# Reordering the turn of a feed-forward stage and taking the second stage's row sums in attention

## The reference

```python
x = x + 0.5 * ffn(layernorm(x))
x = x + attention(layernorm(x))       # causal softmax of |q.k|/16
x = x + 0.5 * ffn(layernorm(x))

def ffn(x):                           # the same weights in both stages
    m = k0 * x[row-1] + k1 * x + k2 * x[row+1]
    h = m @ W1[p] + b1[p]             # 9 paths, 64 wide each
    y = h @ W2[p] + b2[p]
    pick = argmax(tanh(m @ Wo1 + bo1) @ Wo2 + bo2)
    return layernorm(x + y[pick]) * gamma + beta
```

## Time and profile before

| | |
|---|---|
| time, median of 3 | 1526.47 us (1524.82 to 1528.2) |
| the profiled execution's own time | 1531.81 us |
| its span, first to last instruction | 1530.0 us |
| mean granted TensorE clock | 0.967 of full |
| busy: PE, DVE, ACT, POOL | 1359.1, 1215.7, 936.8, 306.9 us |
| chain that ended last: PE, DVE, DMA, ACT | 62%, 11%, 10%, 6% |

### The profile page before, as it was taken

The page is one execution under the profiler, slowest core; times in us unless marked ns, Lnnn a source line. Parts: engine busy times, 40 slices in busy tenths (PEclk is TensorE's granted clock), DMA queues, the critical chain, the costliest instruction groups (busy, mean ns, idle before and its releaser), DMA issues.

```text
span 1530.0 us, 25980 instructions
## 1 busy us (share of the span) xinstructions
PE 1359.1 (89%) x7700; PEld 781.4 (51%) x7700; DVE 1215.7 (79%) x2349; ACT 936.8 (61%) x1745; POOL 306.9 (20%) x359
## 2 busy tenths in 40 slices
PE   4889988858999999999968999999998779989985
PEld 2556666544554454545344455454444346656653
DVE  6989999766677677677866767777678769999985
ACT  5656665326567666566855666766666666666642
POOL 2244452332001000000041101000000214444311
PEclk9989999979999999999989999999999879999997
DMA  5143333320000100102110011000103112333221
GB/s 155 43 118 88 90 101 113 90 69 1 28 29 15 41 14 15 32 11 74 37 43 1 28 42 42 0 28 0 42 0 110 56 32 61 103 97 106 61 74 57
DMA packets 86994, 82.26 MB, mean 54 GB/s; under 512 B 8540, under 2 KB 86885, under 8 KB 86885
## 3 DMA queue, kind: packets, MB, share of 16 engines
q1 hardware_dynamic: 86884, 80.91, 17.8%
HBM read 55.43 MB, written 25.46 MB: 53 GB/s over the span
## 4 chain that ended last, share of the span: by engine, by line
PE 62%; DVE 11%; DMA 10%; issue 7%; ACT 6%; SPq 2%; POOL 1%; DVEq 0%; ACTq 0%; POOLq 0%
PE PS L1324 55%; DMA R<-oh_scratch 7%; PE PS L1501 3%; DMA oh_scratch<-oh_t 2%; DVE R L753 2%; PE PS L1389 2%; PE PS L1332 1%; DVE R L770 1%; DVE R L937 1%; SPq L414 1%; SPq L412 1%; ACT oh_t L1113 1%; ACT R L1211 1%; ACT R L1215 1%; ACT R L1174 1%
## 5 line engine op out<-in xcount | busy, mean ns | idle before, releaser
L1324 PE MATMUL PS<-R 128*128 128x512 f16 (+3 forms) x3456 | 713.6, 361 | 27.4 <-DVE R L937 17.3
L1324 PEld LDWEIGHTS PS<-R 128*128 128x128 f16 (+1 forms) x3456 | 326.0, 98 | 392.3 <-DVE R L937 32.0
L1324 PE MATMUL PS<-w_hi,R 128*128 128x256 f16 x1280 | 239.1, 280 | 63.3 <-DVE R L753 63.1
L937 DVE TENSOR_TENSOR R<-R 128x512 f16<-128x512 f32 (+3 forms) x288 | 188.6, 655 | 111.5 <-ACT R L1215 110.3
L1202 ACT ACTIVATE R<-PS 128x512 f32 (+5 forms) x288 | 160.2, 558 | 162.7 <-PE PS L1324 162.2
L1324 PE MATMUL PS<-R,w_hi 128*128 128x512 f16 x640 | 198.0, 392 | 1.6 <-DVE R L747 1.5
L1211 ACT ACTIVATE R<-R 128x512 f32 (+4 forms) x288 | 169.5, 589 | 48.3 <-DVE R L931 46.8
L931 DVE TENSOR_TENSOR R<-R,max_row 128x512 f32 (+4 forms) x288 | 187.1, 650 | 7.7 <-ACT max_row L1248 7.7
L1215 ACT ACTIVATE R<-R 128x512 f16<-128x512 f32 (+3 forms) x288 | 171.1, 594 | 28.6 <-ACT R L1211 2.6
L925 DVE TENSOR_TENSOR run_max<-run_max,R 128x512 f32<-128x512 f32 (+3 forms) x272 | 173.9, 639 | 10.0 <-DVE run_max L925 1.7
L1324 PEld LDWEIGHTS PS<-w_hi,R 128*128 128x128 f16 x1280 | 128.4, 100 | 104.5 <-DVE R L753 77.1
(11 more groups left out here) (109 smaller groups left out, 1555.3 us busy)
## 6 DMA issues: line engine op xcount, KB each, us to landing
R<-x_scratch SPq DMA_DIRECT2D x48, 512.0 KB, 4.5
x_scratch<-R SPq DMA_DIRECT2D x32, 512.0 KB, 3.2
R<-oh_scratch SPq DMA_DIRECT2D x32, 320.0 KB
R<-in_L_attn_x SPq DMA_DIRECT2D x16, 512.0 KB, 5.4
R<-oh_scratch SPq DMA_DIRECT2D x32, 256.0 KB
out<-R SPq DMA_DIRECT2D x16, 512.0 KB, 3.2
R<-in_L_ffn_W SPq DMA_DIRECT2D x2, 288.0 KB
R<-in_L_ffn_W SPq DMA_DIRECT2D x1, 512.0 KB
```

The lines of the kernel that those rows point to most:

```text
L937: v.tensor_tensor(p_lo[:, i * TT + lo:(i + 1) * TT], pf[:, (i % 2) * TT + lo:(i % 2 + 1) * TT], p_hi[:, i * TT + lo:(i + 1) * TT], ALU.sub ...
L1324: ins = t_.matmul(dst, w, xx, start=start and n == 0, stop=stop and n == last, skip_group_check=skip)
```

## The change

There are three edits.

1. The turn of a feed-forward stage is written in another order on every engine. The router's hidden product moves to the end of the turn before (`FIRST = ROUTE + 1`), so `route` is first on TensorE, and the five route steps on VectorE follow `result`, with the mixing passes between them. The masking of chunks 0, 1, 2 and 3 comes behind the route, each low half two chunks later. In the first stage the input sums stand in the middle of the turn. On ScalarE `scores` goes ahead of `middle`, and `one_hot` ahead of `x_high` and the masked high halves.
2. `residual` on GpSimd is for tile t instead of t+1, stands first in the turn, and waits for the paths of the tile before (`o_psum`) instead of for `masked`.
3. The sums of the second feed-forward stage's input rows are taken in attention (`output_sums`, one or two behind each `output`), into a buffer of their own, `x2_st`; the stage's turns only make the moments from them.

The masks get two semaphores, one for each of the two buffers.

```diff
+FIRST = ROUTE + 1
 # order of the hidden products
-                h_order += [(use(ph, t + ROUTE), 0)] if on(t + ROUTE) else []
                 h_order += [(use(ph, t + HIDDEN), c) for c in range(1, HC)] if on(t + HIDDEN) else []
+                h_order += [(use(ph, t + FIRST), 0)] if on(t + FIRST) else []
 # GpSimd, residual(t) and turn(t)
-                    pool.wait_ge(hm_done, HC * k + 4)
+                    if t >= 1:
+                        pool.wait_ge(o_psum, k)
...
+                    if on(t):
+                        residual(t)
                     if on(t - 1):
                         result_scale(t - 1)
-                    if on(t + HIDDEN):
-                        residual(t + HIDDEN)
 # VectorE, turn(t): the order after the change
+    result(t-1); route 0; mixed_before 0; route 1; mixed_before 1; route 2
+    mixed_behind 0; route 3; mixed_behind 1; route 4
+    masked 0; masked 1; input_sum x4 (first stage only); masked 2; mixed_low
+    masked 3; masked_low 0; masked 4; input_moments or first_stats
+    result_scaled(t-1); masked_low 1; masked_low 2; result_added(t-1)
 # and before
-    result(t-1); masked 0; masked 1; mixed_before 0; mixed_before 1; route 0
-    masked_low 0; route 1; masked 2; route 2; mixed_behind 0; route 3
-    mixed_behind 1; route 4; masked 3; input_sums or first_stats; mixed_low
-    masked 4; input_moments; masked_low 1; result_scaled(t-1); masked_low 2
-    result_added(t-1)
 # ScalarE, turn(t): after
+    scores; middle; squares; normalised; one_hot; x_high
+    masked_high 0; masked_high 1; masked_high 2; transposed
 # and before
-    middle; scores; masked_high 0; squares; normalised; x_high; one_hot
-    masked_high 1; transposed; masked_high 2
 # TensorE, turn(t): after
+    route(t+2); hidden(t+1, 1); path 0; hidden 2; path 1; choice(t+2); hidden 3
+    path 2; hidden 4; path 3; transposed(t+5); hidden(t+3, 0); path 4
 # and before
-    hidden(t+2, 0); hidden(t+1, 1); path 0; route(t+2); hidden 2; path 1
-    hidden 3; path 2; choice(t+2); transposed(t+5); hidden 4; path 3; path 4
 # VectorE, moments in the second stage, and output in attention
+                    dve.wait_ge(x2_sums, SUB * NTT)
+                    dve.wait_ge(n_shift, n - 1)
+                    for u in range(SUB):
+                        ins = v.bn_aggr(mv[:, rows_set(ph, t), u, :], sums_at(t, u))
...
+                    if u >= 1:
+                        output_sums(s, u - 1, rows)
+                    if u == SUB - 1:
+                        output_sums(s, u, rows)
+
+                def output_sums(s, u, rows):
+                    dve.wait_ge(x2_done, SUB * s + u + 1)
+                    v.bn_stats(sums_at(s, u), cols(rows, u * D, D)).then_inc(x2_sums, 1)
 # SyncE stores a row of attention, and TensorE, ScalarE and GpSimd start the
 # second stage, once x2_sums (before: x2_done) is complete
-            wait_apart(eng, x2_done, SUB * NTT)
+            wait_apart(eng, x2_sums, SUB * NTT)
```

## The result

The change made the kernel slower: 1533.15 us (median of 20 runs, 1529.82 to 1536.7) against 1527.12 for the kernel before on the same chip (20 runs, 1522.04 to 1536.35). The ratio is 1.0035, 95% interval 1.002 to 1.005. The forecast was 11.3 us less and the measured change is 6.0 us more, so 17 us are missing.

What follows compares the result with a forecast made beforehand. VectorE was taken to bound the feed-forward turns, TensorE attention. Stage one -1.0, attention +5 and stage two -15.3 sum to -11.3 us: 1515 against the median 1526.5, range 1490 to 1533.

Steps and rivals of the forecast that it cites:

- Bounds and hold: Feed-forward turns are bound by VectorE; residual's hold moves from mixed_low to the first mixed_before, costing 1.63 us.
- Is such a SCALAR_TENSOR_TENSOR held as the TENSOR_TENSOR was?: Whether residual holds the first mixed_before at the turn's start; taken as held, 1.63 us, bounds 0 and 2.36.
- The first: Rival: the first mixed_before is not held by residual, turns near 15.65 to 15.9 us, 1492 us in all; 14%.
- the second: Rival: residual gets the ports between two masked lows, L811 or L770 waits 2.3 us, 1538 us; 9%.
- The third: Rival: attention's sums lie on the path, two thirds of 21 us, no gain in starts, 1527 us; 11%.
- order alone saves only the 0.16 gap: VectorE's turn: the work is the same, so reordering removes only the 0.16 us gap before masked 3.
- The start gains about 1 net: Start of stage one: masks no longer bind, less 1 to 2 us lost in the first routing turn.
- -2.5: Start of stage two: the first path starts 2 to 3 us earlier, as VectorE routes instead of awaiting the mask.
- gain about 1 each: Stage one's two last turns with a residual: no mix to be held back, about 1 us less each.
- attention +5: Sums moved into attention: mostly hidden behind TensorE, +5 us with address arithmetic, bounds +1.6 and +21.
- the third rival's sign: TensorE's waits for L937 and L931 growing at attention's diagonals would show the sums on the path.

Runs made afterwards that it cites:

- experiment 1: The changed kernel with GpSimd's residual(t) moved behind result_scale(t-1) and waiting for masked(t+1, 0) instead of o_psum: 1512.82 us, ratio 0.9912.
- experiment 12: The changed kernel with first_stats in mid-turn instead of behind masked 4, in turns 11 to 15 of the first stage: 1526.71 us, ratio 0.9985.
- experiment 2: The changed kernel with the filling turns (t < 0) of both stages in the old order on VectorE, ScalarE and TensorE: 1526.37 us, ratio 0.9991.
- experiment 7: The changed kernel with residual behind masked(t+1, 0), stage two's sums back in its turns, and filling turns in the old order: 1503.0 us, ratio 0.9831.
- experiment 11: The changed kernel with, in filling turns only, middle ahead of scores and both mixed_before ahead of route step 0: 1528.03 us, ratio 0.9996.
- experiment 6: The changed kernel with residual behind masked(t+1, 0) and the third edit undone (stage two's sums back in its turns): 1509.03 us, ratio 0.9876.
- experiment 10: The changed kernel with useless matmuls added on TensorE at stage one's end, ahead of path(14, 0) and path(15, 0): 1531.98 us, ratio 1.0018.
- experiment 4: The changed kernel without its third edit: the second stage's sums taken in its turns again, none in attention: 1530.44 us, ratio 1.002.
- experiment 5: The kernel before with the third edit alone: sums in attention, none in the second stage's turns: 1533.97 us, ratio 1.0062.
- experiment 8: The changed kernel with useless matmuls added on TensorE in the idle time of the second stage's filling turns: 1528.66 us, ratio 1.0002.
- experiment 3: The changed kernel with turns 13 to 16 of both stages in the old order: 1532.8 us, ratio 1.003.
- experiment 13: The kernel before with residual(t+1) waiting for the last route step of tile t+2 instead of masked(t+1, 3): 1516.73 us, ratio 0.9904.

## Why the prediction was wrong

**Bounds and hold: right.** VectorE bound the turns, the hold moved from `mixed_low` to L752, and its size was 1.44 for 1.63. The prediction asked "Is such a SCALAR_TENSOR_TENSOR held as the TENSOR_TENSOR was?", and the answer is yes: L752 goes from 0.74 to 2.18 with `residual` at the turn's start, and back to 0.73 with it elsewhere (experiment 1). The Trainium skill says so in "SBUF — State Buffer", "Who interferes with whom", and this trace agrees. The steady turns gained 4 to 5 us more than the sum said.

**Rivals.** The first (L752 not held) did not occur. Nor did the second (`residual` getting the ports between the masked lows), but experiment 12 shows one much like it: there `residual` started inside one turn, beside `result_scaled`, and cost it 2.2 us. The third, attention's sums on the path, came in part: 7.4 us instead of 14. The time lies 0.15 above the upper end of the range, 1533, and there by other terms than those that the range was made of.

**Step "order alone saves only the 0.16 gap": failed at the ends.** The work being the same makes order free only where the queue never runs dry. In the filling turns it does: experiments 2, 7 and 11 show 5 to 7 us by their medians for the new order of these turns, in 11 for the routing put ahead of the mixing alone, where the terms "The start gains about 1 net" and, for stage two, -2.5 stood. Traces place only 4 of it (2.0 in each start, experiment 7 against 6). I had seen that `middle` stands behind `scores` and L732 behind the route, and priced it at 1 to 2 us once, with a gain against it from the mask's wait of 6.04 us. That wait is gone after, but the 4.40 us ahead of the first route step took its place.

**Term "gain about 1 each", for the last turns: wrong sign in stage one.** I let only `residual` change in those turns and overlooked that `first_stats` had moved from mid-turn to behind `masked` 4, which the diff says. From result(11) to result(15) the change cost 5.1 instead of -2; experiment 12 gives 6.4 back. About 2.5 of the longest turn are TensorE's lower clock, to which it fell while it was idle for 4.4 us ahead of path(14, 0) (0.71 over the turn, 0.92 in experiment 10). In it also `residual`, moved to the turn's start, holds a one-input TENSOR_SCALAR of six columns, L662: 1.77 us beside `residual`, which runs from 315.26 to 317.60, and 0.16 before. The same section of the Trainium skill names `tensor_scalar` among the forms that can take the shared ports; the trace agrees.

**Term "attention +5": mis-sized,** 7.4 measured; experiments 4 and 5 show that it is all the sums. The six new waits for the column maximum came as forecast, 4.2 us for the 3.4 that were taken; the part that was missing is the 2.1 us more for the low halves of the probabilities, which the prediction had named as the third rival's sign and priced at nothing in its sum.

**What the prediction didn't ask:** what the sums were covering. It subtracted 1.31 a turn and counted the new hold separately, right for this order; but in an order where `residual` lies beside the sums they cost next to nothing (0.01 in a turn of experiment 5, 0.15 in one of experiment 6). So the third edit could only win where the second had put `residual` in the wrong place.

Still open: where the rest of the medians' 5 to 7 us in the filling turns lies, whether the clock at stage two's end is chance in experiments 4 and 8, and how experiment 3 lost 3.7 us there.

## What to carry to other kernels

An order of work that is neutral in the steady turn must be priced again for the filling and the draining turns, instruction by instruction: there each engine waits, and what is queued behind the first wait is late. Where a GpSimd pass over SBUF must run beside VectorE, put it beside instructions that kept their time here: those with a PSUM operand and the batch-norm sums (the one-input TENSOR_SCALAR L662 did not). Before taking such instructions out of a turn, ask what they cover. Moving `residual` alone won 20 us on the changed kernel (experiment 1) and 12 on the kernel before (experiment 13).

## What the runs showed of the hardware

The hold doesn't depend on the size of what is held: a route step of 128x36 with two SBUF inputs (L804, 0.18 elsewhere) took 1.90 us beside `residual` in the first stage's end, while the batch-norm sums beside it in experiment 1 kept their 1.39.

```profile
279.68 2.35 POOL L558 TENSOR_TENSOR R<-R,beta_b 128x1024 f32<-128x1024 f32 x1
```

```profile
280.19 1.90 DVE L804 TENSOR_TENSOR r_pr<-r_eq,prio 128x36 f32<-128x36 f32 x1
```
